# Rank-64 attention factors and split one-pass products for the experts of a one-core transformer layer

## The reference

```
n = layernorm(x)
theta, phi, g = n @ W_theta.T, n @ W_phi.T, n @ W_g.T      # 64, 64 and 256 wide
x = x + (theta @ phi.T / 16) @ g
h = rmsnorm(layernorm(x), ln1_w)
q, k, v = rope(h @ wqkv.T)                                  # 16 heads, 4 key heads, 16 channels
x2 = layernorm(x) + softmax(causal(q @ k.T) / 4) @ v @ wo.T
h2 = rmsnorm(x2, ln2_w)
top two of softmax(h2 @ gate_w.T), their weights made to sum to 1
for e in range(8):
    out += (silu(h2 @ w1[e].T) * (h2 @ w3[e].T)) @ w2[e].T * weight[:, e]   # 512 wide inside
x = x + x2 + out
```

## Time and profile before

| what | us |
|---|---|
| median of 3 runs (1073.9 to 1074.64) | 1074.35 |
| the profiled execution, its own time | 1073.06 |
| its span, first to last instruction | 1071.3 |
| TensorE busy | 1031.6 |
| VectorE busy | 759.7 |
| ScalarE busy | 581.3 |
| GpSimd busy | 417.8 |

### The profile page before, as it was taken

How to read it: one execution, slowest core, us unless ns; L and a number is a source line. 1 busy time by engine, 2 the same in 40 slices (tenths; PEclk the granted TensorE clock), 3 DMA queues, 4 the chain that set the end, 5 groups by cost and what they waited for, 6 DMA issues and landing times.

```text
span 1071.3 us, 19642 instructions
## 1 busy us (share of the span) xinstructions
PE 1031.6 (96%) x6546; PEld 609.5 (57%) x6546; DVE 759.7 (71%) x1811; ACT 581.3 (54%) x1124; POOL 417.8 (39%) x493
## 2 busy tenths in 40 slices
PE   7999899999999899999999999999999999999996
PEld 6766345654444333343333544456668976779995
DVE  5699988787887987899977788333494555655552
ACT  3564577547666888659665566563322344543220
POOL 2020432144743144322444514545637734443332
PEclk9999999999999999999999999999999999999999
DMA  6425122212415666644241332224344422222332
GB/s 195 125 86 156 44 71 88 71 63 69 132 57 147 205 182 202 190 116 115 83 128 64 113 104 52 66 62 90 94 89 109 91 50 45 37 40 40 51 44 23
DMA packets 85731, 101.49 MB, mean 95 GB/s; under 512 B 17632, under 2 KB 73312, under 8 KB 85632
## 3 DMA queue, kind: packets, MB, share of 16 engines
q1 hardware_dynamic: 70752, 80.60, 25.8%
q0 software_dynamic: 14880, 19.64, 9.9%
HBM read 55.76 MB, written 41.14 MB: 90 GB/s over the span
## 4 chain that ended last, share of the span: by engine, by line
PE 75%; DVE 16%; ACT 5%; issue 2%; DMA 1%; POOL 0%; SPq 0%; POOLq 0%; DVEq 0%; ACTq 0%
PE psum L2218 12%; PE psum L2170 10%; PE psum L2240 9%; PE psum L2156 8%; PE psum L2203 7%; DVE psum L1932 5%; PE psum L2136 5%; PE psum L2177 3%; PE psum L2212 3%; PE psum L2122 3%; PE psum L2139 2%; DVE mx L1934 2%; PE psum L2143 2%; ACT probs_mem L1411 2%; PE psum L2067 2%
## 5 line engine op out<-in xcount | busy, mean ns | idle before, releaser
L1411 ACT ACTIVATE probs_mem<-psum 128x512 f32<-128x512 f32 (+1 forms) x464 | 232.6, 594 | 82.7 <-PE psum L2156 81.9
L1932 DVE CUSTOM_DVE_ANT_1 psum<-psum,masking 128x640 f32<-128x640 f32 (+3 forms) x256 | 256.9, 1046 | 25.9 <-PE psum L2139 24.4
L1310 POOL DMA_INDIRECT out<-yout,labels x68 | 108.9, 1601 | 173.5 <-DVE yout L2012 83.5
L2156 PE MATMUL psum<-stack_mem 98*128 98x512 bf16 (+3 forms) x768 | 168.4, 328 | 7.3 <-ACT probs_mem L1411 2.9
L1251 POOL TENSOR_SCALAR_AFFINE_SELECT probs_mem<-probs_mem 128x512 f32<-128x512 f32 x104 | 68.1, 657 | 229.3 <-ACT probs_mem L1411 229.2
L1436 ACT ACTIVATE gated<-psum 128x512 f32<-128x512 f32 x68 | 40.6, 597 | 154.4 <-PE psum L2218 70.2
L2156 PEld LDWEIGHTS psum<-stack_mem 98*128 98x128 bf16 x768 | 65.5, 98 | 102.6 <-ACT probs_mem L1411 23.5
L2170 PE MATMUL psum<-probs_mem,v 128*17 128x512 f32 (+3 forms) x1152 | 117.2, 491 | 0.7 <-ACT heads_out L1418 0.5
L2240 PE MATMUL psum<-w_mem,gated 128*128 x480 | 114.5, 382 | 0.1
L1934 DVE TENSOR_REDUCE mx<-psum 128x4 f32<-128x512 f32 (+2 forms) x96 | 95.7, 1037 | 9.2 <-PE psum L2144 6.7
L2240 PEld LDWEIGHTS psum<-w_mem,gated 128*128 128x128 f32 x480 | 88.0, 190 | 23.8 <-issue 13.7
(11 more groups left out here) (243 smaller groups left out, 1779.8 us busy)
## 6 DMA issues: line engine op xcount, KB each, us to landing
block<-routed SPq DMA_DIRECT2D x68, 129.0 KB, 2.2
w_mem<-in_w13T SPq DMA_DIRECT2D x16, 512.0 KB, 5.6
qk_parts<-w_mem SPq DMA_DIRECT2D x16, 384.0 KB, 2.6
stack_mem<-qk_parts SPq DMA_DIRECT2D x32, 192.0 KB, 3.2
w_mem<-in_x SPq DMA_DIRECT2D x8, 512.0 KB, 5.6
out<-w_mem SPq DMA_DIRECT2D x8, 512.0 KB, 3.7
x_late<-out SPq DMA_DIRECT2D x8, 512.0 KB, 4.9
stack_mem<-qk_parts SPq DMA_DIRECT2D x32, 128.0 KB, 2.8
```

What stands on the lines that cost most here:

```text
L1310: e.indirect_dma_start(out_rows, bass.IndirectOffsetOnAxis(ap=to, axis=0), youts[w % NYOUT], None, bounds_check=NBATCH * SEQ - 1, oob_is_e ...
L1411: e.activation(probs[probs_of(m)][:, hh:hh + n, q0:CH], grid(turn[step][0][:, 0:n * (CH - q0)], n), ACT.Exp, scale=float(HD) ** -0.5).then ...
L1932: e.tensor_tensor_reduce(keys, keys, masked(w), 1.0, -3e38, ALU.add, ALU.max, to).then_inc(sem["max"], 1)
L2156: m = e.matmul(bk[:, i * (CH - q0):(i + 1) * (CH - q0)], s[0:STACK + NMAX, kt // TPR, GRP, kt % TPR * P:(kt % TPR + 1) * P], s[0:STACK + N ...
```

## The change

**Rank-64 factors.** `pair` is gone. The first `square` now multiplies `gram` by W_phi, laid out twice to 128 columns (four products of 128 columns), the second multiplies the result by W_g (two products of 256 columns). A new step `theta` multiplies the transposed rows by W_theta, in two halves of 64 columns of the array (four products of 512 columns). `x1` has four steps of two products that have 64 rows of the array each and write two PSUM banks; a step gives a tile of the first half of the batch and one of the second.

**Joined norm chains.** For batches 1 to 3 `norm1` and `norm2` run once over eight tiles instead of twice over four.

**Experts.** The mixed blocks are gone: the last batch ends in 30 blocks, 71 in all. The staging copies are gone. Instead values are split into a part rounded to the type float32r (`hi`) and the rest (`lo`), and a product is made of three float32r products: hi by hi, hi by lo, lo by hi. The weights `w13` are split once for all blocks, in four quarters, from block 13, 14, 20 and 21 on: ScalarE writes `w13_hi` (16 copies of 1024 columns), VectorE writes `w13_lo` over the old weights (8 instructions of 2048 columns), each after the last block that reads the quarter unsplit. `w2` is split for each block from block 20 on (ScalarE `w2_hi`, VectorE `w2_lo`), as are the rows (`x_hi`, `x_lo`, from block 13) and `gated` transposed (`g_hi`, `g_lo`, from block 20). `w2_lo`, `g_hi` and `g_lo` have one buffer each, which is free when the `down` before is done. All blocks use `gatedT`. ScalarE instead of VectorE scales the result into `yout`.

**Order.** `NUDGE` is a new table, and `LIKE` and `AHEAD` change. Buffers move in memory. The routing of the last batch loses the steps for half blocks.

```diff
-        blocks.append(-(-((n + NE * (HB - 1)) // HB) // 2) if gi == LAST else -(-(n - NE * (P - 1)) // P))
+        blocks.append((n + NE * (P - 1)) // P if gi == LAST else -(-(n - NE * (P - 1)) // P))
...
+SPLIT_FROM = {(0, 0): 13, (1, 0): 14, (0, 1): 20, (1, 1): 21}
+QUARTERS = tuple(SPLIT_FROM)
+LO_PARTS = (slice(0, NE // 2), slice(NE // 2, NE))
+
+DOWN_FROM = 20
...
+def norm_parts(b):
+
+    return 1 if b else 2
...
-TURN, LIKE = 0.1, (2.9, 0.02)
+TURN, LIKE = 0.1, (3.1, 0.06)
...
-AHEAD = {"DVE": 1.7, "ACT": 2.2}
+AHEAD = {"DVE": 1.7, "ACT": 1.9}
...
-        "aggr": {(2,): -33.6},
...
+        "aggr": {(0,): -126.5},
...
-            steps += [("up", w, 0)] * (w < n) + [("gatedT", w - 1)] * (0 < w <= STAGED or mixed(w - 1)) + [("blockT", w + 1)] * (w + 1 < n)
-            steps += [("up", w, 1)] * (w < n) + [("down", w - 1)] * (w > 0)
+            steps += [("gatedT", w - 1)] * (w > 0) + [("up", w, 0)] * (w < n)
+            steps += [("up", w, 1)] * (w < n) + [("blockT", w + 1)] * (w + 1 < n) + [("down", w - 1)] * (w > 0)
...
-                    e.activation((gw, mix)[at[1]], grid(turn[step][0], KD), ACT.Copy).then_inc(sem["square_out"], 1)
+                    if at[1]:
+                        e.activation(outer, turn[step][0][:, 0:D], ACT.Copy).then_inc(sem["square_out"], 1)
+                    else:
+                        e.activation(inner, grid(turn[step][0][:, 0:KD * P], KD), ACT.Copy, scale=float(D) ** -0.5).then_inc(sem["square_out"], 1)
+                elif stage == "theta":
+                    b, = at
+                    q.wait_ge("theta_mm", b + 1)
+                    e.activation(theta_s, turn[step][0], ACT.Copy).then_inc(sem["theta_out"], 1)
...
+                elif stage == "down":
+                    w, = at
+                    q.wait_ge("down_mm", w + 1)
+                    q.wait_ge("add_out", 16 * (w - NYOUT + 1))
+                    q.wait_ge("label", w + 1)
+                    e.activation(youts[w % NYOUT], turn[step][0][:, 0:D], ACT.Copy, scale=labels[w % NLABEL][:, 1:2]).then_inc(sem["y"], 1)
...
+                elif stage == "blockT":
+                    w, = at
+                    q.wait_ge("blockT_mm", w + 1)
...
+                    e.activation(x_hi[w % 2], grid(turn[step][0][:, 0:KD * P], KD), ACT.Copy).then_inc(sem["x_hi"], 1)
...
+                elif stage == "w13_hi":
+                    k, ex = at
+                    of = slice(ex * 2 * FFN, (ex + 1) * 2 * FFN)
...
+                    e.activation(w13_hi[k][:, of], w13_s[:, k, of], ACT.Copy).then_inc(sem["w13_hi"], 1)
...
+                    if w >= DOWN_FROM:
+                        q.wait_ge("down_mm", w)
+                        e.activation(g_hi, turn[step][0], ACT.Copy).then_inc(sem["g_hi"], 1)
+                    else:
+                        q.wait_ge("down_mm", w - 1)
+                        e.activation(gatedT[w % 2], turn[step][0], ACT.Copy).then_inc(sem["gatedT_out"], 1)
...
+                elif stage == "w2_hi":
+                    w, = at
...
+                    at_w = e.value_load(bexp[gi][0:1, c:c + 1], min_val=0, max_val=(NE - 1) * 2 * FFN)
+                    e.activation(w2_hi[w % 2], w2_mem[:, bass.ds(at_w, KF * D)], ACT.Copy).then_inc(sem["w2_hi"], 1)
...
-                    e.tensor_copy(blockT[w % 2], grid(turn[step][0][:, 0:KD * P], KD)).then_inc(sem["blockT_out"], 1)
+                    got = grid(turn[step][0][:, 0:KD * P], KD)
+                    if has_split(w):
+                        q.wait_ge("x_hi", w - min(SPLIT_FROM.values()) + 1)
+                    if has_raw(w):
+                        e.tensor_copy(blockT[w % 2], got).then_inc(sem["x_raw" if has_split(w) else "blockT_out"], 1)
+                    if has_split(w):
+                        e.tensor_tensor(x_lo[w % 2], got, x_hi[w % 2], ALU.subtract).then_inc(sem["blockT_out"], 1)
+                elif stage == "gatedT":
+                    w, = at
+                    q.wait_ge("g_hi", w - DOWN_FROM + 1)
+                    e.tensor_tensor(g_lo, turn[step][0], g_hi, ALU.subtract).then_inc(sem["g_lo"], 1)
+                elif stage == "w2_lo":
+                    w, = at
+                    gi, c = WORK[w]
+                    q.wait_ge("route", routed(gi, "all"))
+                    q.wait_ge("w2_hi", w - DOWN_FROM + 1)
+                    if w > DOWN_FROM:
+                        q.wait_ge("down_mm", w)
+                    at_w = e.value_load(bexp[gi][0:1, c:c + 1], min_val=0, max_val=(NE - 1) * 2 * FFN)
+                    e.tensor_tensor(w2_lo, w2_mem[:, bass.ds(at_w, KF * D)], w2_hi[w % 2], ALU.subtract).then_inc(sem["w2_lo"], 1)
+                elif stage == "w13_lo":
+                    n, part = at
+                    (half, k), experts = QUARTERS[n], LO_PARTS[part]
+                    q.wait_ge("w13_hi", k * NE + range(NE)[experts][-1] + 1)
+                    q.wait_ge("up_mm", 2 * (SPLIT_FROM[half, k] - 1) + half + 1)
+                    e.tensor_tensor(quarter(w13_lo[:, k], half, experts), quarter(w13_s[:, k], half, experts), quarter(w13_hi[k], half, experts),
+                                    ALU.subtract).then_inc(sem["w13_lo_part" if part else "w13_lo"], 1)
...
-                elif stage == "down":
-                    w, = at
-                    q.wait_ge("down_mm", w + 1)
-                    q.wait_ge("add_out", 16 * adds(w - NYOUT + 1))
-                    q.wait_ge("label", w + 1)
-                    e.tensor_scalar(youts[w % NYOUT], turn[step][0][:, 0:D], labels[w % NLABEL][:, 1:2], None, ALU.mult).then_inc(sem["y"], 1)
...
-                    e.tensor_copy(slots[n % NSLOT][:, 1], w13_s[:, 1, bass.ds(at_w, 2 * FFN)]).then_inc(sem["stage_odd"], 1)
...
-                    lhs, rhs = (pairT, gw) if second else (gram, wgT_s)
                     if second:
                         q.wait_ge("square_out", nth[step] - 1)
...
+                        for k in range(KD):
+                            m = e.matmul(bk[:, 0:D], inner[:, k], wgT_s[:, k], start=(k == 0), stop=(k == KD - 1))
                     else:
                         q.wait_ge("gram_out", b + 1)
...
-                    for r in range(KD):
-                        for k in range(KD):
-                            m = e.matmul(bk[:, r * D:(r + 1) * D], lhs[:, k, r * P:(r + 1) * P], rhs[:, k], start=(k == 0), stop=(k == KD - 1))
...
+                        for r in range(KD):
+                            for k in range(KD):
+                                m = e.matmul(bk[:, r * P:(r + 1) * P], gram[:, k, r * P:(r + 1) * P], phi_s[:, k], start=(k == 0), stop=(k == KD - 1))
                     m.then_inc(sem["square_mm"], 1)
+                elif stage == "theta":
+                    b, = at
+                    q.wait_ge("xnT_out", TPB // 2 * (b + 1))
...
+                    for k in range(KD):
+                        for i in range(2):
+                            m = e.matmul(bk[i * LATENT:(i + 1) * LATENT], wtheta_s[:, k], xnT[b % 2][:, k, i * CH:(i + 1) * CH], start=(k == 0), stop=(k == KD - 1))
+                    m.then_inc(sem["theta_mm"], 1)
                 elif stage == "x1":
-                    b, i = at
-                    q.wait_ge("square_out", KD * (b + 1))
-                    q.wait_ge("xnT_out", TPB // 2 * (b + 1))
-                    for c in range(2):
-                        j = 2 * i + c
-                        for k in range(KD):
-                            m = e.matmul(bk[:, c * D:(c + 1) * D], xnT[b % 2][:, k, j * P:(j + 1) * P], mix[:, k], start=(k == 0), stop=(k == KD - 1))
+                    b, j = at
+                    q.wait_ge("square_out", 2 * (b + 1))
+                    q.wait_ge("theta_out", b + 1)
+                    for i in range(2):
+                        rows_of = slice(i * LATENT, (i + 1) * LATENT)
+                        m = e.matmul(bk[:, i * CH:i * CH + D], theta_s[rows_of, j * P:(j + 1) * P], outer[rows_of], start=True, stop=True)
                     m.then_inc(sem["x1_mm"], 1)
...
-                    if w < STAGED:
-                        for k in range(KD):
-                            m = e.matmul(bk, blockT[w % 2][:, k], w13_s[:, k, bass.ds(offset[w] + half * FFN, FFN)],
-                                         start=(k == 0), stop=(k == KD - 1))
-                    else:
-                        q.wait_ge("stage_even", copies_of(w)[-1] + 1)
-                        q.wait_ge("stage_odd", copies_of(w)[-1] + 1)
...
-                    elif w >= STAGED:
-
-                        for c in range(KF):
-                            for k in range(KD):
-                                m = e.matmul(bk[:, c * P:(c + 1) * P], slots[copies_of(w)[0] % NSLOT][:, k, half * FFN + c * P:half * FFN + (c + 1) * P], blockT[w % 2][:, k],
-                                             start=(k == 0), stop=(k == KD - 1))
+                    of = bass.ds(offset[w] + half * FFN, FFN)
+                    if has_raw(w) and has_split(w):
```

(25 more changed lines are left out.)

606 lines of the change are left out of this document (260 added, 346 removed).

## The result

The changed kernel takes **1058.5 us** (median of 4 runs, 1057.8 to 1058.8), the kernel before 1074.5 beside it: ratio 0.984, interval 0.983 to 0.986. That is 16 us less where the prediction had 38 less. The time lies inside its range, but at the price of the rivals, not at that of its sum.

The account below looks back on a forecast made before the run. The prediction took TensorE's work to bound the kernel. Its terms, -14 + 0 - 41 + 9 + 8 = -38, gave a span of 1033.3 us; 1.76 and 1.3 on top made 1036 us, range 1018 to 1064.

Parts of the forecast that it names:

- What bounds the kernel before: Late blocks and second attention: TensorE's work sets the time; early blocks cost 5.83 us of it, late ones 5.52.
- two floors just above it: Late blocks: the serial adds and the loop through ScalarE, both at 4.72 us, against TensorE's 4.56.
- Rank-64 factors, -14: Attention: cheaper TensorE products save 13 us in batches 1 to 3 and 1 in batch 0; range -6 to -18.
- the joined chains, 0: Norms of batches 1 to 3: 15 us less VectorE work, hidden behind TensorE, worth 0 (-5 to +3).
- rival C: Attention: TensorE's saved 13 us turn into waits for VectorE's maxima; 1049, up to 1055 us; chance 0.12.
- Experts, TensorE alone, -41: Expert blocks: TensorE's sum falls from 388 to 347 us, with float32r products at 0.215 and 0.11 us.
- Rival D: Split up and down: a float32r product is not one pass; 1242 us, gain gone at 0.255 a product; chance 0.06.
- The other lists, +9: Blocks from 21 on: VectorE, adds and the ScalarE loop raise the period from 4.56 to 4.75 us; +8 to +25.
- The turn, +8: Blocks where up weights turn to split ones: writing w13_lo over the old weights holds up TensorE; +2 to +14.
- Rival B: Late blocks: the loop through ScalarE is longer, period 5.2 to 5.3 us; 1060 us; chance 0.17.

Follow-up runs that it names:

- theta_twice: Changed kernel with the four products of theta done twice in each batch, same result: ratio 0.990 to the kernel before.
- raw_down: Changed kernel with the split of down undone, float32 in every block: ratio 0.978 to the kernel before.
- raw_up: Changed kernel with the split of up undone, float32 in every block, down still split from block 20: ratio 0.997 to the kernel before.
- addr_early: Changed kernel with TensorE's load of a block's weight address put ahead of the gatedT wait, from block 22 on: ratio 0.967 to the kernel before.
- best2: Changed kernel with the address load moved ahead and the last batch's weight copy moved later, products still float32r: 1042.8 us, ratio 0.964 to the kernel before.
- minus1: Changed kernel with one of the twelve up products left out from block 24 on: ratio 0.979 to the kernel before.
- minus4: Changed kernel with four of the twelve up products left out from block 24 on: ratio 0.968 to the kernel before.
- bf16_up: Changed kernel with the split parts of the up weights and rows in bfloat16 instead of float32r: ratio 0.975 to the kernel before.
- best1: Changed kernel with the address load moved ahead, the last batch's weight copy moved later, and split up and down products in bfloat16: ratio 0.972 to the kernel before.

## Why the prediction was wrong

**What bounds the kernel before** was read rightly, and that TensorE's time counts in the attention holds after the change too (theta_twice). For the late blocks of the changed kernel the prediction took TensorE's list with two floors just above it. Both floors are there, but the loop that decides is longer than the one it counted.

**Rank-64 factors, -14, and the joined chains, 0.** The last `pv` was forecast to end near 686 and ends at 684.7: rival C falls. The parts fit too: `theta` and two groups of `x1` in the changed kernel,

```profile
207.28 1.94 PE L2082 MATMUL psum<-w_mem 128*64 128x512 f32 x8
209.15 0.39 PE L2137 MATMUL psum<-stack_mem 96*128 96x512 bf16 x1
...
218.30 0.70 PE L2090 MATMUL psum<-w_mem 64*128 64x256 f32 x4
218.93 1.09 PE L2097 MATMUL psum<-ident,w_mem 128*128 128x128 f32 x8
```

`theta` takes 1.87, as counted. A pair of `x1` takes 0.63 with its turn, so 2.5 a batch for the 1.8 and up to four turns of 0.13, 2.3. One after the other the two would stream for 0.86 (four records of half of 0.43), so the row halves do run side by side, as the Trainium skill has it ("TensorE: Matmul & The Clock Gate", "Part 3: Packing small matmuls"). The switch of mode that the Trainium skill speaks of ("TensorEngine Tiling (Array Packing)", "Key Properties") is at most the 0.20 beside the 0.43, 0.07 more than a plain turn. Yet that the sum of the stage came out is partly luck: chains and table are worth more than the zero I gave them, and the table of before had its worth as well. How the 25 us divide stays open.

**Experts, TensorE alone, -41: terms that failed in size.** The step took 0.215 and 0.11 for float32r because "its shape is the same". The rows after have 0.232 and 0.119, and the first product of each group 0.1 more. A late block is `up` 2.87 for 2.58, `blockT` and `down` 1.65 for 1.54, and from `gatedT` to `up` 0.35 for 0.44: 4.87, not 4.56, which is 15 us for 47 blocks. Rival D had the right question; its break-even of 0.255 was not reached.

**The other lists, +9: the step that failed.** The prediction closed its loop through ScalarE at `g_lo` and `down`: 3.2 + 1.32 + 0.2 = 4.72. Of what stands behind `g_lo` it said that both products of `gated` "have 0.1 us to spare before TensorE wants them". That step is wrong. The products must be there not only before `gatedT`; behind their wait TensorE's queue also has the address load, and `up` starts 1.23 us after them. So the loop runs on, from `g_lo` (3.09 for 3.2) over both products (1.39) and the load to `up` and the next `down`, 10.25 us for two blocks, 5.13 each: 0.26 above TensorE's own 4.87. The prediction put a price on the very same load in ScalarE's queue (0.69 us ahead of `w2_hi`) and none on TensorE's, though the order of the changed kernel, printed ahead of the prediction, shows it there, behind the transposes. In the early blocks of before it stood behind the transposes too, and the earlier trace rows has 5.83 with no gap: no splits stood ahead of `gated` there, and `down` took 1.73, as in raw_down. The adds alone (4.7 to 5.0) did not decide: with the load moved the same adds follow at 4.82 on average.

Rival B gave the measured period, 5.2, and nearly the time, 1060. It was right that the series through ScalarE, with no buffer doubled, costs more than priced, but not about how: its mark, a wait for `g_lo` ahead of `down`, is absent, and the series up to `g_lo` was shorter than forecast, not longer.

**The turn, +8.** It was 10.9 us by raw_up, in which the saving of the first split quarters, some 4.6 by my estimate (28 quarters at 0.16), is already counted. So its gross cost is some 15, above its range of 2 to 14, and it is found in the trace: 7.9 of `warm` products, 6.3 of waits, and 1.4 in which seven products at the lower clock took 0.2 more each. The prediction named `warm` products and gaps as the signs of the turn, but priced only the wait for `w13_lo`, which is 0.7. Moving one copy on VectorE (weight_late) takes back 5.

**Where the expected gain went:** 47 x 0.31 = 15 us in products, less the 47 x 0.19 = 9 that had been allowed for a floor; 47 x 0.25 = 12 in the loop with the address load; 2 in single longer blocks; 6 in the turn and tail; 2 won back by the attention. The 12 were free to have: addr_early and best2 get them back, and best2 lands within 6 us of where the prediction had put the changed kernel.

## What to carry to other kernels

When one long instruction becomes several short ones, list every instruction in the engine's queue between its waits, not only those that compute: an address load behind a wait is free as long as the work before it is long, and can become part of the period when that work shrinks. Follow a loop until it comes back to where it started, and count how many blocks that takes. What it passes once in two blocks is worth half its length: a product gave back about half of its 0.23 us. Price a type that no row shows from both sides even when its name promises the faster one, and multiply the uncertainty by its count: 0.017 us a product were 0.2 us in each of fifty blocks.

## What the runs showed of the hardware

- A float32r product of 512 columns takes 0.232 us from start to start, of 256 columns 0.119; bfloat16 in place of the 0.232 takes 0.216. Halving its weights' columns shortens their load from 188 to 134 ns and changes no spacing.
- From the end of VectorE's `gated` to the first dependent product after the transposes: 1.23 us with an address load in between (changed kernel, minus1, minus4, bf16_up), 0.73 without (addr_early, best2).
- Two float32 products of 256 columns in the two row halves of the array take 0.63 us: the 0.43 of one, plus 0.20.
- Behind a gap of 2.3 us, seven products stood 0.43 us apart and not 0.23, at a granted clock of 0.50.
- Adds into DRAM that wait for each other: the last 45 of a kernel start 4.77 (minus4), 4.78 (best2), 4.82 (addr_early) and 4.95 us (best1) apart on average.
